# One-core transformer-like kernel: scattered expert results, halved and alternated GELU layers, earlier loads in the delta net

## The reference

```
x = x + 0.5 * zero_moe(layernorm(x))      # stage 0
x = x + attention(layernorm(x))           # stage 1
x = x + 0.5 * zero_moe(layernorm(x))      # stage 2, weights of stage 0
x = x + 0.5 * gelu_moe(layernorm(x))      # stage 3
x = x + delta_net(layernorm(x))           # stage 4
x = x + 0.5 * gelu_moe(layernorm(x))      # stage 5, weights of stage 3
```

## Time and profile before

| | us |
|---|---|
| median of 3 runs | 2405.76 (2404.11 to 2411.33) |
| the profiled execution's own time | 2403.5 |
| its span | 2401.8 |
| TensorE busy with matmuls | 2025.8 (84%) |
| VectorE busy | 1286.1 (54%) |
| ScalarE busy | 1000.3 (42%) |
| GpSimd busy | 391.6 (16%) |

### The profile page before, as it was taken

The page is one execution under the profiler, slowest core; times in us unless marked ns, Lnnn a source line. Parts: engine busy times, 40 slices in busy tenths (PEclk is TensorE's granted clock), DMA queues, the critical chain, the costliest instruction groups (busy, mean ns, idle before and its releaser), DMA issues. The chain is left out here.

```text
span 2401.8 us, 52328 instructions
## 1 busy us (share of the span) xinstructions
PE 2025.8 (84%) x20606; PEld 1490.4 (62%) x20606; DVE 1286.1 (54%) x2928; ACT 1000.3 (42%) x2476; POOL 391.6 (16%) x442
## 2 busy tenths in 40 slices
PE   7889898788626689999999999999999998858884
PEld 4544455677514467767776776777677667638774
DVE  4435444212234576777667767766776776431222
ACT  2114421222113445664665566556546654512221
POOL 0002100200200122212221222122122212202102
PEclk9969998899856899999999999999999999958997
DMA  1100003710101111011101110110111010045001
GB/s 46 33 13 1 15 26 105 250 31 21 44 11 45 30 31 24 18 35 24 33 20 37 24 33 20 33 27 18 35 24 33 20 28 11 11 164 187 27 21 62
DMA packets 148345, 100.08 MB, mean 42 GB/s; under 512 B 88640, under 2 KB 134992, under 8 KB 148112
## 3 DMA queue, kind: packets, MB, share of 16 engines
q1 hardware_dynamic: 144368, 86.59, 12.8%
q0 software_dynamic: 3744, 10.23, 1.5%
HBM read 83.28 MB, written 13.50 MB: 40 GB/s over the span
## 5 line engine op out<-in xcount | busy, mean ns | idle before, releaser
L1589 PE MATMUL dn_ps<-xnT,dn_w 128*128 128x512 f32 x512 | 260.5, 635 | 35.2 <-DMA dn_w<-in_W_qkvz_dram 23.9
L1942 DVE SCALAR_TENSOR_TENSOR dn_cv<-dn_raw,dn_cw,dn_cv 128x1024 f32<-128x1024 f32 x192 | 270.6, 1409 | 1.2
L588 PE MATMUL g_ps<-g_w,xnT 128*128 (+1 forms) x736 | 166.1, 379 | 0.0
L1589 PEld LDWEIGHTS dn_ps<-xnT,dn_w 128*128 128x128 f32 x512 | 91.2, 197 | 116.3 <-issue 100.1
L577 PE MATMUL g_ps<-g_xT,g_w_now 128*128 128x128 f32 x960 | 117.4, 282 | 50.3 <-DVE g_w_now L716 50.3
L1734 PE MATMUL dn_ps<-dn_wout,dn_oT 128*128 128x256 f32 x512 | 150.0, 418 | 6.2 <-ACT dn_oT L1749 3.7
L1749 ACT ACTIVATE dn_kdk<-dn_ps,dn_cf 128x128 f32<-128x128 f32 x256 | 80.2, 364 | 179.3 <-PE dn_ps L1629 179.3
L516 ACT ACTIVATE xnT<-g_ps,g_b_now 128x128 f32<-128x128 f32 x240 | 68.6, 368 | 206.1 <-PE g_ps L577 206.1
L577 PEld LDWEIGHTS g_ps<-g_xT,g_w_now 128*128 128x128 f32 x960 | 112.6, 196 | 61.5 <-issue 61.5
L588 PEld LDWEIGHTS g_ps<-g_w,xnT 128*128 128x128 f32 x736 | 136.4, 190 | 16.7
L1749 ACT ACTIVATE dn_raw<-dn_ps 128x512 f32<-128x512 f32 x128 | 76.6, 598 | 148.7 <-PE dn_ps L1589 148.7
(11 more groups left out here) (309 smaller groups left out, 4413.2 us busy)
## 6 DMA issues: line engine op xcount, KB each, us to landing
g_w<-in_fc_dram SPq DMA_DIRECT2D x32, 1024.0 KB, 13.1
dn_w<-in_W_qkvz_dram SPq DMA_DIRECT2D x16, 768.0 KB, 4.5
dn_x<-dn_cum_rows SPq DMA_DIRECT2D x32, 256.0 KB, 3.9
ys_rows<-g_ys SPq DMA_DIRECT2D x46, 128.0 KB, 1.7
dn_wout<-in_W_out_dram SPq DMA_DIRECT2D x16, 256.0 KB, 2.8
f_gate<-in_gateT_dram SPq DMA_DIRECT2D x16, 128.0 KB, 2.2
f_up<-in_upT_dram SPq DMA_DIRECT2D x16, 128.0 KB, 2.4
f_down<-in_downT_dram SPq DMA_DIRECT2D x16, 128.0 KB, 2.4
```

The lines of the kernel that those rows point to most:

```text
L588: last = pe.matmul(y_b[i % 2][:, 0:D], hT[i % 2][:, f, :], of(f), start=(f == 0), stop=(f == NF - 1))
L1589: mm = pe.matmul(to, w[:, k, W_COL[u] * P:(W_COL[u] + 1) * P], m.xnT[:, k, b * T:(b + 1) * T], start=(k == 0), stop=(k == KD - 1))
L1942: ins = nc.vector.scalar_tensor_tensor(out=cv[:, u], in0=raw[:, u, :, tap:tap + T], scalar=cw[:, g, tap:tap + 1], in1=cv[:, u], op0=ALU.mu ...
```

## The change

In `moe_zero`: `top_two` issues all 8 searches of one kind before it waits, and the zero experts' additions stand behind the loop over the experts.

In `moe_gelu`: a third product (`token[:, :, 2]`) gives for each slot the row of its token and pick; padding gets row 2048 (`SPARE`), which nobody reads. GpSimd writes each result tile with an indirect transfer to those rows (`put_back`), each after the last one has landed, and fetches six tiles ahead in between. When all have landed SP loads the 16 blocks of 128 rows in order. TensorE's order for tile i becomes first half of `first(i)`, first half of `second(i - 1)`, second half of `first(i)`, `turn(i + 2)`, second half of `second(i - 1)`. VectorE's order becomes `copy_w1(i + 1)`, `copy_x(i + 2)`, `copy_y(i - 1)`. The additions of the second bias all stand ahead of the first weighted addition.

In stage 4: the constants and the first head's weights, taps and output weights are loaded by SP inside `delta_gates`, behind its own loads; the delta net's block begins with semaphore increments in their place. The next heads' `w` is loaded in two parts, the first 512 KB after projection 7, the last 256 KB after projection 11.

```diff
@@ top_two
     for t in range(NT):
-        chain(nc.vector.max(m8[:, t, :], scores[:, t, :]))
-        chain(nc.vector.max_index(ix[:, t, :], m8[:, t, :], scores[:, t, :]))
+        nc.vector.max(m8[:, t, :], scores[:, t, :]).then_inc(chain.sem, 1)
+    chain.n += NT
+    chain.eng.wait_ge(chain.sem, chain.base + chain.n)
+    for t in range(NT):
+        nc.vector.max_index(ix[:, t, :], m8[:, t, :], scores[:, t, :]).then_inc(chain.sem, 1)
+    chain.n += NT
+    chain.eng.wait_ge(chain.sem, chain.base + chain.n)
@@ moe_zero, VectorE
-            for t in range(NT):
-                nc.vector.scalar_tensor_tensor(out=m.x[:, t, :], in0=m.xn[:, t, :], scalar=zero_w[:, t:t + 1],
-                                               in1=m.x[:, t, :], op0=ALU.mult, op1=ALU.add).then_inc(chain_sem, 1)
-            dve.wait_ge(chain_sem, chain.n + NT)
+            dve.wait_ge(chain_sem, chain.n)
...
+            dve.wait_ge(acc_done, 2 * UNITS * STEPS + A_FREE)
+            for t in range(NT):
+                nc.vector.scalar_tensor_tensor(out=m.x[:, t, :], in0=m.xn[:, t, :], scalar=zero_w[:, t:t + 1],
+                                               in1=m.x[:, t, :], op0=ALU.mult, op1=ALU.add).then_inc(chain_sem, 1)
+            dve.wait_ge(chain_sem, chain.n + NT)
@@ moe_gelu, SP
-            for i in range(TILES):
-                sp.wait_ge(y_copied, i + 1)
-                sp.dma_start(tile_rows(ys_rows, i), ys[:, i % 3, :]).then_inc(ys_stored[i % 3], 16)
+            sp.wait_ge(y_copied, TILES)
             for n in range(3):
                 sp.wait_ge(ys_stored[n], 16 * ((TILES - n + 2) // 3))
+            for t in range(NT):
+                for r in range(2):
+                    sp.dma_start(gathered[r][:, t, :], tile_rows(ys_rows, r * NT + t)).then_inc(ys_back[t], 16)
@@ moe_gelu, GpSimd
+            def put_back(i):
+                pool.wait_ge(y_copied, i + 1)
+                if i >= 1:
+                    pool.wait_ge(ys_stored[(i - 1) % 3], 16 * ((i + 2) // 3))
+                nc.gpsimd.indirect_dma_start(ys_rows, bass.IndirectOffsetOnAxis(ap=place_u[:, i:i + 1], axis=0),
+                                             ys[:, i % 3, :], None).then_inc(ys_stored[i % 3], 16)
+
+            for i in range(RING):
+                fetch(i)
             pool.wait_ge(place_ready, 1)
-            for n in range(3):
-                pool.wait_ge(ys_stored[n], 16 * ((TILES - n + 2) // 3))
-            for t in range(NT):
-                for r in range(2):
-                    j = r * NT + t
-                    nc.gpsimd.indirect_dma_start(gathered[r][:, t, :], None, ys_rows,
-                                                 bass.IndirectOffsetOnAxis(ap=place_u[:, j:j + 1], axis=0)).then_inc(ys_back[t], 16)
+            for i in range(TILES):
+                if i + RING < TILES:
+                    fetch(i + RING)
+                put_back(i)
@@ moe_gelu, TensorE
             for i in range(TILES):
-                first(i)
+                first(i, 0)
+                if i >= 1:
+                    second(i - 1, 0)
+                first(i, 1)
                 if i + 2 < TILES:
                     turn(i + 2)
                 if i >= 1:
-                    second(i - 1)
-            second(TILES - 1)
+                    second(i - 1, 1)
+            second(TILES - 1, 0)
+            second(TILES - 1, 1)
@@ moe_gelu, VectorE, the rows and the loop
+            nc.vector.tensor_tensor(token[:, :, 2, :], in_tile[:], over_tiles(route[:, R_BACK:R_BACK + 2 * NT]), ALU.mult).then_inc(token_ready, 1)
...
+            chain(nc.vector.scalar_tensor_tensor(out=place_f[:], in0=in_tile[:, 0, :], scalar=float(SPARE), in1=in_tile[:, 1, :],
+                                                 op0=ALU.add, op1=ALU.add))
+            nc.vector.tensor_tensor(place_u[:], place_f[:], in_tile[:, 2, :], ALU.subtract).then_inc(place_ready, 1)
...
             for i in range(TILES):
+                if E1 <= i + 1 < TILES:
+                    copy_w1(i + 1)
                 if i + 2 < TILES:
                     copy_x(i + 2)
                 if i >= 1:
                     copy_y(i - 1)
-                if E1 <= i + 1 < TILES:
-                    copy_w1(i + 1)
@@ delta_net, before delta_gates; called there by SP behind its own loads
+        def load_first(sp, first_loaded):
+            sp.dma_start(w[:], weights_of(0)).then_inc(first_loaded, 16)
+            sp.dma_start(cw[:], taps_of(0)).then_inc(first_loaded, 16)
+            sp.dma_start(wout[:], out_of(0)).then_inc(first_loaded, 16)
...
+            return 8 + LEVELS
@@ delta_net, SP
             def load_weights(kh):
+                wait(sp, "pj", kh * 12 - 4)
+                sp.dma_start(w[:, :, 0:4 * P], weights_of(kh)[:, :, 0:4 * P]).then_inc(w_loaded, 16)
+
+            def load_z_weights(kh):
                 wait(sp, "pj", kh * 12)
-                sp.dma_start(w[:], W_qkvz[:, kh * NCOL:(kh + 1) * NCOL].rearrange("(k p) n -> p k n", p=P)).then_inc(w_loaded, 16)
+                sp.dma_start(w[:, :, 4 * P:NCOL], weights_of(kh)[:, :, 4 * P:NCOL]).then_inc(wz_loaded, 16)
```

More of the change, by code:

```diff
@@ L359, in route_constants @@
     tile = np.tile(P * np.arange(NT), 2).astype(np.float32)
+    back = (SPARE - NTOK * (np.arange(2 * NT) // NT)).astype(np.float32)
     spread = lambda a: np.broadcast_to(a, (P, len(a)))
     part = r[:, None].astype(np.float32)
-    return np.ascontiguousarray(np.concatenate([before, ones, groups, count, spread(rows), part, spread(tile)], axis=1))
+    return np.ascontiguousarray(np.concatenate([before, ones, groups, count, spread(rows), part, spread(tile), spread(back)], axis=1))
 def moe_gelu(nc, m, tag, gate, gate_bias, fc1, fc1_b, fc2, fc2_b, alpha, iota_in, route_in, xn_rows, ys_rows):
@@ L481, in _, with fetch @@
             pool.wait_ge(tokens_ready, 1)
-            for i in range(TILES):
+            def fetch(i):
                 if i >= RING:
@@ L544, in _ @@
                     pe.wait_ge(in_slot_ready, j // 4 + 1)
-                last = pe.matmul(y_b[0][:, 0:2 * TILES], in_slot[:, j, :], token[:, j].rearrange("p a n -> p (a n)"),
+                last = pe.matmul(y_b[0][:, 0:3 * TILES], in_slot[:, j, :], token[:, j].rearrange("p a n -> p (a n)"),
                                  start=(j == 0), stop=(j == 2 * NT - 1))
@@ L559, in turn, with first @@
                 last.then_inc(turned, 1)
-            def first(i):
+            def first(i, half):
                 if i < E1:
@@ L565, in first @@
                 else:
[L566 removed]
+                    if half == 0:
+                        expert[i] = nc.tensor.value_load(owner[0:1, i - E1:i - E1 + 1], min_val=0, max_val=E1 - 1)
                     of = lambda k, f: w1_now[:, f // HT, k, f % HT * P:(f % HT + 1) * P]
                 pe.wait_ge(xT_copied, i + 1)
[L569 to L579 removed]
@@ L581, in second @@
-            def second(i):
+                if i >= 2:
+                    pe.wait_ge(h_ready, 2 * (i - 2) + half + 1)
+                if i >= E1:
+                    pe.wait_ge(w1_copied, 2 * (i - E1) + half + 1)
+                for q in range(HT):
+                    f = half * HT + q
+                    for k in range(KD):
+                        last = pe.matmul(h_b[2 * (i % 2) + half][:, q * P:(q + 1) * P], of(k, f), xT[i % 2][:, k, :],
+                                         start=(k == 0), stop=(k == KD - 1))
@@ L582, in second @@
+                last.then_inc(fc1_ready, 1)
+            def second(i, half):
                 of = (lambda f: w2[:, i, f, :]) if i < E1 else (
                     lambda f: w2[:, bass.ds(expert[i], 1), f, :].rearrange("p a d -> p (a d)"))
-                pe.wait_ge(h_ready, 2 * (i + 1))
-                if i >= 2:
+                pe.wait_ge(h_ready, 2 * i + half + 1)
+                if i >= 2 and half == 0:
                     pe.wait_ge(y_copied, i - 1)
-                for f in range(NF):
+                for f in range(half * HT, (half + 1) * HT):
@@ L588, in second @@
                     last = pe.matmul(y_b[i % 2][:, 0:D], hT[i % 2][:, f, :], of(f), start=(f == 0), stop=(f == NF - 1))
-                last.then_inc(y_ready, 1)
+                if half == 1:
+                    last.then_inc(y_ready, 1)
             turn(0)
@@ L1192, in _ @@
             sp.wait_ge(stored, 16 * 2 * GRP)
+            sp.wait_ge(first_loaded, 16 * first)
         @block.tensor
```

101 lines of the change are left out of this document (53 added, 48 removed).

## The result

The kernel after takes 2321.05 us (median of 4 runs, 2319.36 to 2325.31), the kernel before beside it 2404.94 us: a ratio of 0.9651, with a 95% interval from 0.9626 to 0.9676. The profiled execution took 2319.88 us, with a span of 2318.2; that is 83.6 less than the one before, where the prediction's sum was 93.7. The forecast of 2311 is 10 us too low, and inside its range.

The account below looks back on a forecast made before the run. TensorE's work was taken to bound the delta net, its waits the GELU stages. Terms 60.0 + 19.6 - 1.0 + 0.1 + 6.0 + 9.0 = 93.7 us off 2403.5 gave 2309.8 (2312.1 by median); forecast 2311, range 2302 to 2334.

Parts of the forecast that it names:

- The GELU order: GELU stages: half-layers on TensorE and the weights' copy first on VectorE remove the copy wait; 30.0 us a stage, 60.0 together.
- the read of the register: GELU late tiles: TensorE's read of the expert's number stays hidden, cost 0; rival that it shows: 15 us, 2326, chance 0.11.
- The clock "1.00 throughout": GELU stages: sign of being right, TensorE's granted clock at 1.00 throughout; 0.50 had been seen in the first late tile.
- TensorE busy for 168 us without a break: GELU stage: sign of being right, TensorE unbroken from first tile to last, 168 us instead of 198.
- The way back: GELU stages' end: scattering finished tiles and loading plain blocks saves 9.8 us a stage, 19.6; the routing's extra product costs 1.0.
- T + 15.4: GELU stage's end: the last sum done 15.4 us after T, the end of the last result's copy; 25.2 before.
- rival on the scatter: GELU way back: scatter slow at the end (2331 us, chance 0.12), or its chain the bound (2423 at 9 us landing, 0.03).
- landing of 1.7 us: GELU way back: best case for a scatter's time to land, gaining 11.4 us a stage; 3.0 us was assumed.
- The zero experts: Both zero-expert stages: batched searches remove a 3.38 us TensorE wait, sums at the end cost 3.3; net gain 0.1 us.
- First weights in the gates' stage: Delta net's start: loading the first head's weights during the gates' stage saves 6.0 us, bounds 4 and 7.2.
- Weights in two parts: Delta net: earlier first 512 KB remove the 10.4 us weights wait; gain 9.0 us, between 5 (half passes on) and 10.4.
- the delta net gives nothing back: Delta net: rival that its small waits pass to the state's chain and its start is bound otherwise; 15 lost, 2326, chance 0.12.

Follow-up runs that it names:

- late_first: The kernel after, with the first head's loads issued only when the gates' own loads have landed: 2315.08 us, ratio to before 0.9617.
- whole_rows: The kernel after, with the gates' two small vectors loaded as whole 128-byte rows to all partitions, VectorE picking each head's elements: 2303.81 us.
- all_three: The kernel after with late_first, whole_rows and the zero experts' sums inside the expert loop (two per pass) joined: 2290.68 us, ratio to before 0.951.

## Why the prediction was right or wrong

**The GELU order: 60.0 predicted, 58.9 measured.** The period of a late tile is 7.25 us, the wait for the copy is 0, the read of the register costs nothing. The price was right and so was the reading of the waits; which of the two edits earns it the prediction left open, and it is the copy's place alone. Its own timetable held the answer: a copy at 1.9 to 2.6 for a first layer at 7.25 fits with whole layers too.

**The clock "1.00 throughout" came but for the first tile.** The granted clock in the second GELU stage is 0.87 in the mean because of the routing ahead of the loop and the first 3.8 us of the first tile. From 2131.1 on it is 1.00, and a late tile's half takes 1.78 us. The other sign, TensorE busy for 168 us without a break, came as 164.6.

**The way back: 19.6 less 1.0 predicted, 17.5 measured alone,** 19.3 by the stages of the profiled execution. T + 15.4 came as T + 15.3. That it fits so closely is partly luck, for the mechanism was half right: SP's issues come every 0.47 us, not 0.57, and are done at T + 11.4; the end is set by VectorE's sums at 0.52 each, which in the kernel after run without a pause from 2303.80. The prediction had named them as a second path that ends at about the same time. Neither rival on the scatter came: 3.11 us at the end, at most 5.7, below the 6.55 at which its chain would decide. The Trainium skill (DMA: Bandwidth & Descriptors, Anatomy of one DMA) says that the receipt of a write is heaviest when the target is HBM. This case again does not show it: in the kernel after the gathers take 3.2 us and the scatters 2.4 in the median from 2126 to 2200, 3.8 and 2.7 from 2200 to 2270. (In the prediction the gain for a landing of 1.7 us should be 11.1 us a stage, not 11.4; that changes nothing in the sum and less than 1 us in the range.)

**The zero experts: 0.1 predicted, 0.8 measured alone,** within the noise.

**First weights in the gates' stage: 6.0 predicted, 1.2 measured.** This is the step whose mechanism failed. The gain at the delta net's start came: the first matmul 1.9 us after the memset instead of 8.4, the decay rows' first use 4.5 instead of 10.5. But I had priced the loads in the gates' stage at nothing, since they "stand behind those on SP's queue and have the rest of that stage". They stand behind them on SP's queue, but they are not without effect on them: the first product there starts 3.2 to 4 us later, and the stage grows by 3 to 5; `late_first` gives both back. That the DMA engines are what the two share is my reading, which no run isolates. The row that should have warned me is TensorE's wait of 18.35 us for a 4 KB transfer. I took it as cover and did not ask what kept that transfer. The Trainium skill (DMA: Bandwidth & Descriptors, Queues, rings and completion order) says that data descriptors are no barrier to each other and only the completion's write is ordered behind all earlier ones of the engine. The runs show less than that: the transfer issued first was in 24.7 us after its issue began with others issued behind it (kernel after), 20.3 without (`late_first`); whether any data overtook other data no trace here shows.

**Weights in two parts: 9.0 predicted, 2.2 measured alone,** about 3 by the stretches of fourteen kernels. Two things in this term were mis-sized. The wait for `dn_w` did go, but its 10.4 us were one execution's; seven kernels have 8.3 in the mean. And most of it passed on: TensorE's wait for `dn_wv` rose by 5.8 to 5.9, which is 70% and not the half that I had as the worst. 8.3 less 5.8 is 2.5, and that accounts for what was measured. The lower bound of 5 was too high, and the sign that I had named, a wait in the state's chain that grows as `dn_w`'s shrinks, came for the most part; for this term the rival "the delta net gives nothing back" was nearer than the forecast. The kernel after saved 12.0 us in the delta net in its profiled execution; about 6.4 of them are the start. The other 5.6 are more than the 3 of the fourteen, and the execution before, with the longest wait for `dn_w`, is one reason.

**Stages 0 to 2, 3.3 us,** no term of the sum (2.8 of them in the second zero-expert stage): the executions differ in how long the clock stays low, with the same code.

What each part gives alone adds up to 80.6 us, the whole change to 83.9. Each of the small ones is uncertain by 3 to 4 us and the large ones by 5 to 7, so I don't read anything into the difference. The whole came out inside the range because the two large terms were right; the two in stage 4 were not, 15.0 predicted and 3.4 measured alone.

## What to carry to other kernels

When an in-order engine feeds the one that sets the end, look first at what stands ahead of the awaited instruction in its queue: here the place of one copy was worth 59 us, and a finer interleaving on the engine that waited was worth nothing. A load that is moved into an idle stretch can't be counted as free when something in that stretch is itself waiting for a transfer; here it cost 3 to 5 us. Issue it after that transfer has landed, and ask why that wait is there at all. A wait that is taken away can pass to the next engine in the chain, here 70% of it, and its size in one profiled execution can be the high one: look at several. Loading the same two small vectors in another form was worth 17 us, more than either of the two edits around it.

## What the runs showed of the hardware

Four transfers of 4 KB, made of 1024 elements of 4 bytes each, hold SP's queue for 0.7 to 7.5 us an issue, and the last is in 20.3 us after its issue began (`late_first`, from 635.29 to 655.55). The same values as rows of 128 bytes (two transfers of 16 KB, `whole_rows`) take 0.43 us an issue. The Trainium skill (DMA: Bandwidth & Descriptors, Specifications) says that a transfer below 512 bytes becomes a read-modify-write; these runs show that small elements are slow, but not that this is why, since rows of 128 bytes are below that as well.

The first head's 768 KB take 15.9 us from issue to landing behind those elements in the kernel after, and 4.3 to 5.3 us where none are in flight (`late_first`, `all_three`, `whole_rows`).

The clock's low stretches differ between executions with the same code: 13.7 to 23.9 us of the second zero-expert stage, with 107.7 to 111.4 us of length, and 25.3 to 48.8 us of the delta net's inner stretch. A single pair of profiled executions can't be read for less than a few us. The Trainium skill (TensorE: Matmul & The Clock Gate, What's actually happening) says that one kernel gives different counts of slow matmuls in different runs, and these runs agree.
